# An attention and mixture-of-experts block on one core: preceding sums added by a transfer, values projected as three fp32r products

## The reference, cut to what matters

```python
xn = layernorm(x)
shifted = xn one step later (zero at the start of a sequence)
k, v, r = (xn*mix_j + shifted*(1-mix_j)) @ W_j.T          # j = k, v, r
# for each channel, over time: w = -exp(time_decay), u = time_first
out = (e1*num + e2*v) / (e1*den + e2)                     # num, den: decayed sums over the steps before
num, den = e1s*num + e2s*v, e1s*den + e2s                 # with a running maximum taken out of all exps
x1 = x + layernorm((sigmoid(r) * out) @ Wo.T)
y = shared(h) + routed(h), h = layernorm(x1)              # relu squared MLP of width 1024; 6 of 64 experts, capacity 128
result = x1 + layernorm(y)
```

## Time and profile before

| | us |
|---|---|
| runs before, median of 3 (lowest, highest) | 1229.62 (1229.37, 1231.83) |
| span of the profiled execution | 1230.5 |
| TensorE busy | 1125.4 (91%) |
| VectorE busy | 868.8 (71%) |
| ScalarE busy | 727.4 (59%) |
| GpSimd busy | 300.0 (24%) |

### The profile page before, as it was taken

The page is one execution under the profiler, slowest core; times in us unless marked ns, Lnnn a source line. Parts: engine busy times, 40 slices in busy tenths (PEclk is TensorE's granted clock), DMA queues, the critical chain, the costliest instruction groups (busy, mean ns, idle before and its releaser), DMA issues.

```text
span 1230.5 us, 15805 instructions
## 1 busy us (share of the span) xinstructions
PE 1125.4 (91%) x5208; PEld 811.8 (66%) x5208; DVE 868.8 (71%) x1984; ACT 727.4 (59%) x1250; POOL 300.0 (24%) x264
## 2 busy tenths in 40 slices
PE   5988999999999986889999889999998999999894
PEld 3635455454545444668888778888887887878761
DVE  4699999999999989599888844544454444444385
ACT  2666779788888888733332245665565555546353
POOL 2010202122020101100000035424433453434246
PEclk9999999999999987889999999999999999999898
DMA  8401033150303225765452079979988988887799
GB/s 318 177 7 35 5 99 78 60 137 34 103 35 69 77 61 171 169 233 193 148 201 81 5 232 260 250 238 250 255 229 255 254 239 250 230 228 181 185 319 354
DMA packets 79538, 206.23 MB, mean 168 GB/s; under 512 B 10209, under 2 KB 10337, under 8 KB 76641
## 3 DMA queue, kind: packets, MB, share of 16 engines
q1 hardware_dynamic: 59424, 156.98, 36.3%
q0 software_dynamic: 20032, 48.24, 20.5%
HBM read 145.93 MB, written 59.28 MB: 167 GB/s over the span
## 4 chain that ended last, share of the span: by engine, by line
PE 33%; DMA 11%; DVE 8%; issue 3%; POOL 2%; ACT 2%; POOLq 0%; DVEq 0%; ACTq 0%
DMA ysh<-k_sb,mixf 8%; PE bank L713 6%; PE bank L688 3%; PE bank L690 3%; PE bank L689 3%; PE bank L670 3%; PE bank L672 3%; PE bank L671 3%; DMA xres<-h,mixf 2%; PE bank L728 2%; PE bank L702 2%; PE bank L729 2%; PE bank L730 1%; DVE stats L1879 1%; PE bank L524 1%
## 5 line engine op out<-in xcount | busy, mean ns | idle before, releaser
L577 PE MATMUL bank<-mix_ring,weights 128*128 128x512 f32 x512 | 224.4, 595 | 2.8 <-ACT k_sb L829 2.8
L577 PEld LDWEIGHTS bank<-mix_ring,weights 128*128 128x128 f32 x512 | 97.6, 191 | 123.2 <-issue 118.2
L1338 POOL DMA_INDIRECT ysh<-k_sb,mixf x64 | 113.5, 1773 | 201.9 <-DMA ysh<-k_sb,mixf 108.3
L584 PE MATMUL bank<-weights,rw 128*128 128x512 f32 x256 | 119.0, 621 | 9.9 <-DVE rw L1491 5.5
L1100 ACT ACTIVATE k_sb<-bank 128x512 f32<-128x512 f32 x64 | 38.2, 597 | 143.9 <-PE bank L672 140.5
L1796 DVE TENSOR_TENSOR run_max<-run_max 128x256 f32<-128x256 f32 x64 | 27.3, 426 | 117.4 <-ACT e_split L1136 117.4
L1314 POOL DMA_INDIRECT xres<-h,mixf x48 | 53.6, 1117 | 221.0 <-DVE mixf L1782 210.3
L670 PE MATMUL bank<-h_high,ffn_w 128*128 128x512 f32 x256 | 103.3, 403 | 2.7 <-ACT k_sb L1100 2.7
L688 PE MATMUL bank<-ffn_w,s_split 128*128 128x512 f32 x256 | 102.5, 401 | 1.8 <-DVE s_split L1775 1.8
L1802 DVE TENSOR_TENSOR wkv_split<-wkv,xnd_split 128x1024 fp32r<-128x1024 f32 x48 | 58.9, 1227 | 61.8 <-ACT xnd_split L1144 61.8
L671 PE MATMUL bank<-h_low,ffn_w 128*128 128x512 f32 x256 | 101.1, 395 | 0.0
(11 more groups left out here) (244 smaller groups left out, 2550.9 us busy)
## 6 DMA issues: line engine op xcount, KB each, us to landing
wkv<-in_w SPq DMA_DIRECT2D x96, 512.0 KB
state<-in_w SPq DMA_DIRECT2D x32, 512.0 KB
xin<-h SPq DMA_DIRECT2D x8, 1024.0 KB, 6.7
xin<-in_x SPq DMA_DIRECT2D x7, 1024.0 KB, 7.3
xres<-in_x POOLq DMA_DIRECT2D x7, 1024.0 KB, 9.4
x<-xres SPq DMA_DIRECT2D x7, 1024.0 KB, 4.8
h<-hb SPq DMA_DIRECT2D x7, 1024.0 KB, 4.5
ht<-xnT SPq DMA_DIRECT2D x7, 1024.0 KB, 8.7
```

Of the source, the lines that this page charges most:

```text
L577: mm = pe.matmul(bank[:, d, :], W(j)[:, ck, d * P:(d + 1) * P], mix_slot(4 * j + ck), start=(ck == 0), stop=(ck == CK - 1))
L584: mm = pe.matmul(bank[:, s, :], rw[:, ck, s * P:(s + 1) * P], W(3)[:, ck, :], start=(ck == 0), stop=(ck == CK - 1))
L1338: pool.indirect_dma_start(t["ysh"], bass.IndirectOffsetOnAxis(ap=scatter_token[:, e % IB:e % IB + 1], axis=0), e_out[q], None, compute_op= ...
```

## The change

- The sums of the preceding columns are no longer added by VectorE. Once num_scan of a chunk is done, POOL issues one transfer of 128 x 2 x 512 fp32 (512 KB) from `recur` that adds them into NUM and R, made neighbours in `unit` for this (`add_prev`). Everyone who waited for den_ready or num_ready waits for it (`prev_in`). The last chunk of the last tile keeps the two adds.
- The gap k minus maximum goes to VE's place instead of G's. In `exps` the Relu into R comes after the Exp of E1 and E2 and waits for rw_ready of two chunks before.
- Values of tiles 1 to 7 are projected as three fp32r products like the receptance: the high weights lie over hb, the low ones over Wv; new are wv_round and v_round on ScalarE, wv_rest and v_rest on VectorE.
- hb being taken, h is made in place in xres: ln3_normalise waits for the x1 store, y_scaled for the h store, x1 is stored a period earlier and x1_squares(tau-1) moves into period tau. The blank rows come from xres. `hots` waits for the last projection.
- VectorE's gaps, scans and refine are cut in pieces and interleaved with pieces of other chunks and with mixes; ScalarE's, POOL's and SP's lists are put in a new order; x is loaded for tau+3. Some semaphores are merged.

The lists of the periods are written out short in the diff, several calls to a line.

```diff
-R, E1, E2, G, NUM, VE = range(6)
+NUM, R, E1, E2, G, VE = range(6)
+GAP = VE
+        wv_hi = sb("wv_hi", [P, CK, C], F32R, over="hb")
+        def by_dma(u):
+            return u < CK * NT - 1
+        def prev_in(eng, u, sums):
+            if by_dma(u):
+                eng.wait_ge(S[f"prev_added{u % 2}"], 16 * (u // 2 + 1))
+            else:
+                eng.wait_ge(S["sums_added"], sums)
...
 # TensorE
+            def project_v(bank, tau, ck):
+                pe.wait_ge(S["v_lo_ready"], CK * (tau - 1) + ck + 2)
+                project_split(bank, wv_hi, wv_lo, v_high(tau, ck), low(VJ, ck), ck)
-                        project(even, tau + 1, VJ, ck)
+                        project_v(even, tau + 1, ck)
...
 # ScalarE
+            def v_round(tau, ck):
+                act.wait_ge(S["mixed"], 12 * tau + 4 * VJ + ck + 1)
+                if ck == CK - 1:
+                    act.wait_ge(S["mix_used"], 12 * tau + 4 * VJ + 1)
+                else:
+                    act.wait_ge(S["mix_used"], 12 * (tau - 1) + 4 * RJ + ck + 2)
+                act.activation(v_high(tau, ck), mix_slot(4 * VJ + ck), ACT.Copy).then_inc(S["v_hi_ready"], 1)
             def exps(tau, c):
...
                 act.activation(unit[:, b, E1:E2 + 1, :], unit[:, b, E1:E2 + 1, :], ACT.Exp, scale=-1.0).then_inc(S["exped"], 1)
+                if u >= 2:
+                    act.wait_ge(S["rw_ready"], u - 1)
+                act.activation(unit[:, b, R, :], unit[:, b, GAP, :], ACT.Relu, bias=vecs[:, ROOM, c:c + 1], scale=-1.0).then_inc(S["lifted"], 1)
...
 # ScalarE, period after
+                if here:
+                    if has(tau, -2):
+                        ln3_normalise(tau - 2)
+                    if last(tau):
+                        ffn_round(0)
+                    exps(tau, 1)
+                    recip(tau, 0)
+                    carry_over(tau, 0)
+                    seed(tau, 2)
+                    if ahead: v_round(tau + 1, 0..2)
+                    if has(tau, 2):
+                        ln1_normalise(tau + 2)
+                    if ahead:
+                        k_read(even, tau + 1, 1 - par)
+                    if first(tau):
+                        ffn_round(1)
+                    exps(tau, 2)
+                    if behind:
+                        y_squares(odd, tau - 1)
+                    if ahead:
+                        v_round(tau + 1, CK - 1)
+                    recip(tau, 1)
+                    carry_over(tau, 1)
+                    seed(tau, 3)
+                    if ahead: r_round(tau + 1, 0)
+                    if last(tau): h_copy(0..3)
+                    if behind:
+                        y_scaled(odd, tau - 1)
+                    if ahead: r_round(tau + 1, 1); v_read(even, tau + 1, 0..3); r_round(tau + 1, 2)
+                    exps(tau, 3)
+                    if has(tau, 2): xnT_read(even, tau + 2, 0..3)
+                    if ahead: r_round(tau + 1, CK - 1)
+                    recip(tau, 2)
+                    carry_over(tau, 2)
+                    if last(tau): scores(turn_bank, 0); exp_table(); h_hi(0, 0); h_hi(0, 1); sd_high(0)
+                    if behind and ahead:
+                        x1_squares(tau - 1)
+                    if ahead: seed(tau + 1, 0); exps(tau + 1, 0); r_read(odd, tau + 1, 0..3); exp_table()
+                    if ahead: carry_over(tau, 3); seed(tau + 1, 1)
+                    recip(tau, 3)
...
 # GpSimd
+            def add_prev(tau, c):
+                u = CK * tau + c
+                pool.wait_ge(S["r_times_v"], u + 1)
+                pool.wait_ge(S["scanned"], 2 * u + 2)
+                pool.dma_start(unit[:, c % 2, NUM:R + 1, :], sums_of[:, c % 2, :, 0:TT], accum_op=ALU.add).then_inc(S[f"prev_added{u % 2}"], 16)
 # its period after: scale_and_offset(1, tau+2), add_prev 0, add_prev 1, ln2_inv_std(tau-1), add_prev 2, add_residual(tau-1), add_prev 3, ln3_inv_std(tau-1)
...
 # SP, period after: store_h(tau-2), load_x(tau+3), (last: load_h(1), sd load), store_x1(tau-1), (last: sd load)
...
 # VectorE, start and period after (seen as one line a group)
+            centre_wo(); wv_rest(); shift(1, 1); diff(1, 0..3); mix(1, KJ, 0..3)
+            ln1_moments(tau+2)    # period 0: behind mixes(RJ, 0)
+            den_scan 0, r_times_v 0, num_scan 0, gap_scan 1, mixes(VJ, 0), gap_taken 1, recip_used(tau-1, 3), mixes(VJ, 1), refined(tau-1, 3), mixes(VJ, 2, 3), mixes(RJ, 0)
+            den_scan 1, v_rest 0, r_times_v 1, v_rest 1, num_scan 1, gap_scan 2, num_gated 0, gap_taken 2, recip_used 0, mixes(RJ, 1), refined 0, v_rest 2, mixes(RJ, 2)
+            den_scan 2, v_rest 3, r_times_v 2, r_rest 0, num_scan 2, gap_scan 3, num_gated 1, gap_taken 3, recip_used 1, mixes(RJ, 3), refined 1, shift, r_rest 1, 2, diff 0, 1
+            den_scan 3, r_rest 3, r_times_v 3, mix(tau+2, KJ, 0), num_scan 3, gap_scan(tau+1, 0), num_gated 2, gap_taken(tau+1, 0), recip_used 2, mix KJ 1, refined 2, diff 2, 3, mix KJ 2, 3, num_gated 3
...
                 if first(r):
-                    dve.wait_ge(S["h_stored"], 16 * (NT - 1))
+                    dve.wait_ge(S["mix_used"], 12 * NT)
```

More of the change, by code:

```diff
@@ L347, in period @@
                 if has(tau, -2):
-                    store_tail(tau - 2)
+                    store_h(tau - 2)
+                if has(tau, 3):
+                    load_x(tau + 3)
                 if last(tau):
@@ L352, in period @@
                     load_raw(2)
+                if has(tau, -1) and not behind_all(tau):
+                    store_x1(tau - 1)
+                if last(tau):
                     sp.wait_ge(S["r_times_v"], CK * NT)
@@ new lines, in period @@
+                    if ahead:
+                        r_round(tau + 1, 1)
+                        for c in range(CK):
+                            v_read(even, tau + 1, c)
+                        r_round(tau + 1, 2)
+                    exps(tau, 3)
+                    if has(tau, 2):
+                        xnT_read(even, tau + 2, *range(CK))
+                    if ahead:
+                        r_round(tau + 1, CK - 1)
+                    recip(tau, 2)
+                    carry_over(tau, 2)
@@ new lines, in period @@
+                    if last(tau):
+                        scores(turn_bank, 0)
+                        exp_table()
+                        h_hi(0, 0)
+                        h_hi(0, 1)
+                        sd_high(0)
+                    if behind and ahead:
+                        x1_squares(tau - 1)
+                    if ahead:
+                        seed(tau + 1, 0)
+                        exps(tau + 1, 0)
+                        for c in range(CK):
+                            r_read(odd, tau + 1, c)
+                        exp_table()
+                        carry_over(tau, 3)
+                        seed(tau + 1, 1)
@@ L1302, in period @@
                     sd_rest(1)
-                if has(tau, -1):
+                if here:
+                    add_prev(tau, 2)
+                if behind:
                     add_residual(tau - 1)
+                if has(tau, 1):
+                    add_prev(tau, CK - 1)
+                    if behind:
+                        ln3_inv_std(tau - 1)
             periods(pool, period)
@@ L1701, in mixes, with mixes_next, diffs_next, v_rests @@
                             mix(tau + 1, j, ck)
-                if behind:
-                    refine(tau - 1, 3)
+                def mixes_next(j, *chunks):
+                    if has(tau, 2):
+                        for ck in chunks:
+                            mix(tau + 2, j, ck)
+                def diffs_next(*chunks):
+                    if has(tau, 2):
+                        for ck in chunks:
+                            diff(tau + 2, ck)
+                def v_rests(*chunks):
+                    if ahead:
+                        for ck in chunks:
+                            v_rest(tau + 1, ck)
+                def r_rests(*chunks):
+                    if ahead:
+                        for ck in chunks:
+                            r_rest(tau + 1, ck)
+                if has(tau, 2) and not first(tau):
+                    ln1_moments(tau + 2)
+                if here:
+                    den_scan(tau, 0)
+                    r_times_v(tau, 0)
+                    num_scan(tau, 0)
+                    gap_scan(tau, par, 1)
+                    mixes(VJ, 0)
+                    gap_taken(tau, par, 1)
+                if behind:
+                    recip_used(tau - 1, 3)
+                if here:
+                    mixes(VJ, 1)
+                if behind:
+                    refined(tau - 1, 3)
                 if behind_all(tau):
```

361 lines of the change are left out of this document (181 added, 180 removed).

## The result

The changed kernel takes 1244.45 us (median of 4 runs, 1242.47 to 1250.05) where the kernel before, run beside it, takes 1229.49 (4 runs, 1229.11 to 1231.83): a ratio of 1.012, 95% interval 1.0088 to 1.0152. The direction and the range were both missed. The profiled execution is the slowest of the four, 1250.05 us with a span of 1248.3.

The account below looks back on a forecast made before the run. The longest loop through the queues of three nearly full engines was taken to bound the kernel. Terms -2.4 - 1.9 + 0.2 + 4.4 - 3.6 = -3.3 us gave a median of 1226.3 us, range 1211 to 1239.

Parts of the forecast that it names:

- Work per period: Steady attention period: TensorE saves 2.6 to about 51.4 us, VectorE 51.0, ScalarE 49 busy; all could run in 51.4.
- The loop: Refined of chunk 3, ScalarE's 34.4 us chain, next tile's seed(0), gap_scan(0), 8.0 us to the next moments: period 54.3 to 54.4.
- The transfers: 512 KB sums land in 5.6 us; two places feel it, recip(0) and the residual; period 55.4, 0.5 less than before.
- behind 512 KB of adding it is 0 to 2 us late; I take 1.0: Residual queued on POOL behind the sums of chunk 2: x1_squares on ScalarE waits 1.0 us a period for it.
- (a) recip(0)... 0.3: ScalarE's recip of chunk 0: sums land at T+13.3, ScalarE is there at T+13.0, so 0.3 us of wait a period.
- The laid-out period of 55.4: Steady attention period: loop of 54.3 to 54.4 us with 0.3 for recip(0) in it, and 1.0 for the residual.
- Rival 3: Sums land late at recip(0), each us beyond 5.6 adding to the period six times; at 8 us, 1240.7; chance 0.22.
- Middle: Four steady attention periods, each 0.5 us shorter: -1.9 us.
- Last tile: First product of chunk 0 to last refined grows from 42.6 to 48.5 us, first product 1.5 earlier: +4.4 us.
- Beginning: Start to the receptance of the second period: first scan product at 62.1, receptance at 147.7 instead of 150.0: -2.4 us.
- Start of the FFN: hots(0) no longer waits 6.3 us for the h store: -3.6 us, between 0 and -6.3.
- Blocks over 56.5 us apart: Sign to look for: receptance blocks start 55.4 us apart if the forecast holds, over 56.5 if rival 3 does.

Follow-up runs that it names:

- the kernel of 1219.8 us: Changed kernel with seed(0) ahead of x1_squares, h stores behind chunk 0's sums, four last-tile moves and wv_rest later: 1219.8 us, ratio 0.990 to the kernel before.
- the last experiment: Against the kernel of 1219.8 us: r_read(7) ahead of exps(7,0), both ahead of x1_squares(6), sums of (6,3) on VectorE, h copies and group scores moved: 1218.9 us.

## Why the prediction was wrong, by its steps

**Work per period: right.** 49 us on ScalarE and 51.0 less waits on VectorE were forecast (48.9 and 49.5), and the values' products do start 0.23 us apart. TensorE's saving was put at 2.6 us; at a granted clock of 1.00 it was 54.7 - 52.7 = 2.0 (the second number from the kernel of 1219.8 us).

**The loop: right in its path, and this is what the experiments bear out.** The predicted loop, refined of chunk 3, ScalarE's unbroken chain, seed(0), gap_scan(0), is where the period was set: the seed moved out of x1_squares' shadow gave 3.75 us a period, two us of work off the chain (and 2.5 off VectorE) 2.25, a transfer's wait off it 1.95.

**The transfers: here it failed.** The step "behind 512 KB of adding it is 0 to 2 us late; I take 1.0" measured 2.9, since the residual lands in 12.5 us and not in 9.4 to 11.4. The step "(a) recip(0)... 0.3" measured 1.6, since those sums land in 7.5 and not 5.6. The laid-out period of 55.4 plus 1.9 and 1.3 is 58.6, the measured one. That it closes so well is partly luck: the same layout for all sums on VectorE, 54.4 and four adds of 0.6 in the loop, gives 56.8 against 57.55. No run takes the two waits away and nothing else. The median landing of 5.3 was under the 5.6 that I took. So it was no error in the size of one transfer: I had each of them alone in the DMA queues, although I had written down what runs beside each (the h store at the start of the period, the x load at its end). Of the residual's 12.5, 0.4 could have been read in the kernel before, where it takes 9.8 in these periods and not 9.4; the rest comes from the sums ahead of it, since it lands in 9.3 when it goes first. Rival 3 had the mechanism and the sign, but put all of it on recip(0), and by a slower transfer; the larger half was on the residual, and the transfer by itself is not slow.

**Middle: -1.9 forecast, +10.8 measured**, by those two terms if the layout's sum is right. This is 12.7 of the 18.6 us by which the forecast missed; the last tile is 3.9 and the beginning 2.1.

**Last tile: +4.4 forecast, +8.3 measured.** The chain from the first product to the last refined took 50.8 us where I laid out 48.5. The larger part is the start: "the first product itself comes 1.5 earlier" came 1.2 later behind the receptance block (461.11 - 438.76 = 22.35 against 21.13), as num_gated(6,3) waited 3.26 us for its sums, which landed in 10.4. TensorE's queue, which I had not followed there, waits 11.4 instead of 4.4 for r_read(7), which the change puts behind exps(7,0); but halving that wait in the last experiment brought 0.9 us, so what else holds the last tile stays open.

**Beginning: -2.4 forecast, -0.3 measured.** The first product came at 60.63, 1.5 earlier than laid out, and the gain was lost again in tile 0: ln1_normalise(2) waited 4.22 us for POOL's offsets at 77.89, and TensorE 9.95 for k_read behind it at 82.80. After that its first twelve products started 0.43 us apart. Neither the wait nor the lower clock was in the layout of the first period.

**Start of the FFN: -3.6 forecast, -4.5 measured.** The wait at hots is gone, as said.

**What the forecast said would show.** Blocks over 56.5 us apart: rival 3, and so it was. "The landing of the sums near 5.6 us" was no test of it: the median was 5.3 and the period 58.6 all the same. The row to ask for was the landing of the one transfer that the loop waits for.

## What to carry to other kernels

Where three engines are nearly full, take work off one of them only after finding the loop through their queues: here a split that saves TensorE 2 us and a transfer that saves VectorE 4.7, with the order that came with them, made the kernel 1.2% slower. Moving one tiny seed ahead of work that needs a late transfer cut the period by 3.75 us, and with the smaller moves beside it the same two edits were a gain of 1.0% over the kernel before. What the new order does without either edit no run shows. Price a transfer by what stands ahead of it in its queue and what runs beside it at that moment, for each place that waits for it, never by its median. And when two transfers share a queue, ask for both who waits for them before swapping them.

## What the runs showed of the hardware

An adding transfer of 512 KB from SBUF to SBUF takes 5.0 us at best, and 7.2 to 7.6 where a store of 1 MB is issued 0.3 to 0.6 us behind it; with the store held back it takes 5.1 at that place. Issued 0.8 us behind a 1 MB adding transfer in the same queue it takes 12.2 to 13.7. The 1 MB adding transfer issued 0.8 us behind one of 512 KB lands in 12.5 instead of 9.3, and a plain 1 MB load on the other queue in 9.9 instead of 7.5 where no sums are transferred. An idle stretch of 2 us on TensorE was followed by eight products at half clock (0.43 us apart for 0.23), 1.6 us more; before the change the 1.5 us waits of the earlier trace rows had no such products behind them.
